# A new order of work for a cross-attention and mixture-of-experts attention kernel on one core

## What is computed

```
x = x + cross_attention(layernorm(x), ctx, lens)      # 77 context keys, 16 heads of 32, masked by length
x = x + expert_attention(layernorm(x))                # 512 keys, 16 heads of 32
```

## Time and profile before

| | |
|---|---|
| time, median of 3 runs | 1420.75 us (1419.51 to 1426.21) |
| profiled execution, span | 1426.7 us |
| PE busy | 1391.0 us, 97% of the span, 5704 matmuls |
| PE weight loads busy | 702.4 us, 49% |
| DVE, ACT, POOL busy | 67%, 60%, 48% |
| PE's granted clock, in tenths over 40 slices | 9 or more in all but two, which have 8 |

### The profile page before, as it was taken

The page is one execution under the profiler, slowest core; times in us unless marked ns, Lnnn a source line. Parts: engine busy times, 40 slices in busy tenths (PEclk is TensorE's granted clock), DMA queues, the critical chain, the costliest instruction groups (busy, mean ns, idle before and its releaser), DMA issues.

```text
span 1426.7 us, 17122 instructions
## 1 busy us (share of the span) xinstructions
PE 1391.0 (97%) x5704; PEld 702.4 (49%) x5704; DVE 951.9 (67%) x1687; ACT 861.3 (60%) x1499; POOL 679.8 (48%) x411
## 2 busy tenths in 40 slices
...
GB/s 252 143 53 133 46 68 96 153 76 46 98 110 108 75 54 125 137 61 76 68 111 123 75 59 135 110 85 67 58 104 152 76 46 97 64 101 79 81 39 30
DMA packets 78767, 130.81 MB, mean 92 GB/s; under 512 B 26374, under 2 KB 32134, under 8 KB 75607
## 3 DMA queue, kind: packets, MB, share of 16 engines
...
...
## 4 chain that ended last, share of the span: by engine, by line
PE 85%; ACT 7%; issue 2%; DMA 2%; POOL 2%; DVE 1%; ACTq 0%; SPq 0%; POOLq 0%
PE pj L1217 43%; PE scT L1302 9%; PE sc L1274 8%; PE acc L1331 7%; PE sc L1263 4%; PE pj L1247 2%; PE pj L1311 2%; PE scT L1295 2%; PE pj L1319 2%; PE pj L1340 2%; DMA qs<-shift 2%; PE pj L1190 1%; ACT xhat L810 1%; PE pj L1202 1%; PE pj L1211 1%
## 5 line engine op out<-in xcount | busy, mean ns | idle before, releaser
L925 ACT ACTIVATE probs<-scT 128x512 f32<-128x512 f32 x512 | 288.9, 594 | 303.9 <-PE scT L1302 300.8
L1048 DVE TENSOR_REDUCE negmax<-sc 128x1 f32<-128x512 f32 x512 | 338.0, 684 | 140.7 <-PE sc L1274 139.7
L784 POOL TENSOR_TENSOR probs_sum<-probs_sum,probs 128x1024 f32<-128x1024 f32 x128 | 300.2, 2365 | 57.4 <-ACT probs L925 57.3
L1075 DVE RECIPROCAL inv_sum<-pj 128x128 f32<-128x128 f32 x256 | 225.0, 921 | 59.9 <-PE pj L1340 39.2
L1274 PE MATMUL sc<-ks,qs 96*128 96x512 f32 x512 | 260.1, 541 | 2.4 <-DVE negmax L1048 1.6
L1217 PE MATMUL pj<-XT,Wqk 128*128 128x512 f32 x512 | 257.3, 598 | 0.6 <-DVE Wqk L1140 0.6
L1302 PE MATMUL scT<-qs,ks 99*128 99x512 f32 x512 | 250.9, 517 | 6.2 <-DMA qs<-shift 3.2
L780 POOL TENSOR_TENSOR probs_sum<-probs 128x1024 f32<-128x1024 f32 x64 | 151.4, 2372 | 173.8 <-ACT probs L925 173.8
L790 POOL TENSOR_TENSOR uv_stack<-UVS_sb,uv_stack 96x1024 fp32r<-96x1024 f32 x32 | 75.7, 2367 | 178.1 <-ACT UVS_sb L832 178.1
L1302 PEld LDWEIGHTS scT<-qs,ks 99*128 99x128 f32 x512 | 94.7, 191 | 124.5 <-ACT probs L925 60.4
L754 POOL TENSOR_TENSOR xhat<-xhat,inv_sum 128x128 f32<-128x128 f32 (+1 forms) x56 | 45.1, 806 | 207.7 <-DVE inv_sum L1075 207.7
...
## 6 DMA issues: line engine op xcount, KB each, us to landing
Wqk<-in_WmT SPq DMA_DIRECT2D x16, 1024.0 KB, 6.1
Wvo<-in_WmT SPq DMA_DIRECT2D x16, 1024.0 KB, 6.5
...
qs<-stage_lo SPq DMA_DIRECT2D x136, 64.0 KB, 2.2
qs<-qs SPq DMA_DIRECT2D x34, 256.0 KB, 3.0
X<-in_x SPq DMA_DIRECT2D x8, 1024.0 KB, 6.0
ks<-stage_lo SPq DMA_DIRECT2D x128, 64.0 KB, 2.0
ks<-ks SPq DMA_DIRECT2D x32, 256.0 KB, 3.0
```

The costliest lines, as they stand in the source:

```text
L784: nc.gpsimd.tensor_tensor(probs_sum[:, pair], probs_sum[:, pair], probs[:, kt % 2, pair], ALU.add)\
L925: nc.scalar.activation(probs[:, kt % 2, jj, :], scT[:, ST[step], :], ACT.Exp, scale=SCALE)\
L1048: nc.vector.tensor_reduce(negmax[:, 0, n:n + 1], sc[:, SC[step], :], AX.X, ALU.max, negate=True)\
L1075: nc.vector.reciprocal(inv_sum[:, INV[use], at], pj[:, PJ[left_in(full)], at])\
```

## The change

All numbers of `CALENDAR` and `OWN` are replaced. Everything below them is as it was: the same 3917 steps with the same instructions, the same `PERIOD`, buffers and rules for waits; since waits' values and banks are derived from the order, they follow it. Many of the new places come in pairs or fours a tenth apart, so that like steps stand next to each other. In the list of PE, a `sc` step followed by another `sc` was found 107 times and is now 222 times, `sT` by `sT` 95 and now 224 times, `sc` by `sT` or `sT` by `sc` 316 and now 159 times.

The core of the diff, with the kinds of step that are spoken of below:

```diff
 CALENDAR = {
...
-    "xpose": (-1734, -1732, -1712, -1710, 141, 141, 163, 163),
...
-    "uv_load": (346, 397, 524, 2882),
...
-    "cacc": (-1106, -626, -363, -44),
...
-    "wm_load": (235, 409, 224, 3285),
...
-    "qk_rows": (919, 773, 1317, 1353, 1778, 1739, 2284, 2360),
-    "qk_stack": (1003, 896, 1345, 1373, 1880, 1780, 2418, 2420),
...
-    "shift": (1339, 1901, 2375, 2899),
-    "shift_move": (1367, 1967, 2390, 2987),
...
-    "accout": (2115, 2487, 3005, 3448),
-    "den": (1871, 2376, 2959, 3434),
...
+    "xpose": (-1747.9, -1747.7, -1736.2, -1736.1, 146.2, 146.4, 166.3, 166.4),
...
+    "uv_load": (270.7, 270.8, 426.9, 2579.7),
...
+    "cacc": (-1191.3, -612.8, -383.2, -7.3),
...
+    "wm_load": (170.8, 286.2, 737.4, 3063.8),
...
+    "qk_rows": (866, 751.1, 1362.8, 1386.1, 2035.8, 1786.4, 2294.6, 2348.2),
+    "qk_stack": (866.1, 751.3, 1363, 1386.2, 2035.9, 1786.5, 2294.8, 2376.8),
...
+    "shift": (1437.1, 1944.7, 2368.7, 2831.7),
+    "shift_move": (1437.2, 1944.8, 2368.8, 2831.8),
...
+    "accout": (2117.8, 2526.2, 2900.9, 3459),
+    "den": (1870, 2418.2, 2902.8, 3505.2),
...
 OWN = {
...
-    "gate_hidden": {(0,): 247, (7,): 14443},
-    "gate_top": {(0,): 271, (7,): 14468},
...
-    "warm": {(0, 2): -989, (1, 3): -909, (2, 1): -663, (3, 4): -423, (4, 5): 71, (5, 2): 170, (6, 3): 244,
-        (7, 3): 323, (8, 2): 334, (9, 3): 555, (10, 4): 768},
...
-    "shift": {(7, 0): 15606, (7, 1): 18277, (7, 2): 19738, (7, 3): 20530},
...
-    "den": {(7, 0): 18507, (7, 1): 19738, (7, 2): 20740, (7, 3): 21892},
...
-    "divide": {(7, 0, 0): 18986, (7, 1, 0): 20855, (7, 2, 0): 21354, (7, 3, 0): 22067, (7, 3, 1): 22391,
-        (7, 3, 2): 23543, (7, 3, 3): 24079},
...
+    "warm": {(0, 2): -566.3, (1, 3): -542, (2, 1): -431.4, (3, 4): -374.9, (4, 5): 201.2, (5, 2): 218.8,
+        (6, 3): 181.5, (7, 3): 223.4, (8, 2): 176.1, (9, 3): 749, (10, 4): 684.5},
...
+    "shift": {(7, 0): 15653.5, (7, 1): 18511.1, (7, 2): 19859.8, (7, 3): 20758.4},
...
+    "den": {(7, 0): 18597.2, (7, 1): 20054.2, (7, 2): 21211.5, (7, 3): 22403.8},
...
+    "divide": {(7, 0, 0): 18970.9, (7, 1, 0): 21145, (7, 2, 0): 21799.1, (7, 3, 0): 22404, (7, 3, 1): 22977.8,
+        (7, 3, 2): 23089.1, (7, 3, 3): 23624.1},
+    "gate_hidden": {(0,): 212.4, (7,): 14459.7},
+    "gate_top": {(0,): 239.1, (7,): 14513.3},
```

More of the change, by code:

```diff
@@ L65 @@
-    "cinv": (-946, -942, -933, -931, -536, -530, -527, -519, -427, -408, -392, -304, -29, -17, -9, 19),
-    "wm_load": (235, 409, 224, 3285),
[L67 to L75, removed]
@@ L101 @@
-    "divide": (2251, 2923, 3435, 3454, 3559, 3656, 3896),
-    "out2": (3491, 3507, 3522, 3540, 3721, 3723, 3740, 3766, 3789, 3804, 3826, 3889, 3930, 3941, 3958, 3988),
-    "residual2": (3579, 3916, 3925, 4017),
+    "context": (-2133.4,),
+    "context_v": (-2041.2,),
+    "load": (-1944.5,),
+    "stats": (-1944.4, -1944.3, -1944.2, -1944.1),
+    "deviation": (-1887.7, 74.1),
+    "normalize": (-1786.8, 146.1),
+    "xpose": (-1747.9, -1747.7, -1736.2, -1736.1, 146.2, 146.4, 166.3, 166.4),
@@ new lines @@
+    "q1": (-1642.4, -1642.3, -1642.2, -1642.1, -1639.7, -1639.6, -1621.3, -1557.1, -924, -923.9, -923.8, -923.7,
+        -851.2, -699.1, -649, -648.9),
+    "q1_split": (-1642, -1511.7, -923.6, -648.8),
+    "q1_rows": (-1622.9, -1255.7, -909.5, -434.6),
+    "q1_stack": (-1619.8, -1213.6, -909.4, -319.9),
+    "pick": (270.6,),
+    "uv_load": (270.7, 270.8, 426.9, 2579.7),
+    "csc": (-1483.4, -1446, -1436.3, -1436.2, -1108.2, -1108.1, -1097, -1096.9, -629.1, -620, -589.3, -589.2,
+        -319.8, -319.7, -297.8, -297.7),
@@ new lines @@
+    "cross_shift": (-1387.9, -1037.1, -584.7, -269.6),
+    "cross_shift_move": (-1387.8, -1037, -584.6, -269.5),
+    "csT": (-1262.1, -1262, -1255.9, -1255.8, -933.5, -933.3, -909.7, -909.6, -527, -490.4, -490.3, -434.7, -125.9,
+        -125.8, -99.6, -99.5),
+    "cpv": (-1191.4, -612.9, -383.3, -7.4),
+    "cacc": (-1191.3, -612.8, -383.2, -7.3),
+    "cden": (-933.7, -566.9, -400, 12.1),
+    "cinv": (-933.6, -933.4, -933.2, -933.1, -468.4, -468.3, -468.2, -468.1, -399.9, -399.8, -399.7, -379.2, 54.6,
+        54.7, 55, 55.3),
@@ new lines @@
+    "wm_load": (170.8, 286.2, 737.4, 3063.8),
+    "cdivide": (-484.8, -468, -187.2, 54.8, 54.9, 55.2, 55.6),
+    "out1": (-9.8, -9.7, -9.6, 55.1, 36.1, 36.2, 36.3, 55.5, 62.5, 62.6, 62.7, 62.8, 73.6, 73.7, 73.8, 73.9),
+    "residual1": (55.4, 55.7, 62.9, 74),
+    "residual_bias": (1505.8,),
+    "token_sums": (146.5, 146.6, 166.5, 166.6),
+    "gate_hidden": (234.4,),
+    "gate_top": (270.5,),
+    "gate_scale": (295.8,),
+    "uv_hi": (356.2, 545.5, 607.9, 3138),
+    "uv_lo": (356.3, 545.6, 608, 3138.1),
@@ new lines @@
+    "weff": (461.9, 462, 485.8, 508.4, 595.7, 595.8, 607.7, 607.8, 737.5, 737.6, 737.7, 758.7, 3361.2, 3409.5,
+        3409.6, 3424.2),
+    "qk": (525.2, 536.6, 536.7, 536.8, 617.7, 617.8, 648.2, 677.7, 992.3, 1039.6, 1149.8, 1165.2, 1261.1, 1261.2,
+        1289.7, 1306.6, 1446.6, 1446.7, 1451.2, 1451.3, 1535.9, 1545.5, 1553.3, 1656.1, 2137, 2143.7, 2143.8,
+        2204.6, 2299.1, 2311.9, 2312.1, 2320),
+    "qk_split": (581.6, 677.8, 1292.9, 1306.7, 1451.4, 1701.6, 2204.7, 2328.1),
+    "qk_rows": (866, 751.1, 1362.8, 1386.1, 2035.8, 1786.4, 2294.6, 2348.2),
@@ new lines @@
+    "accout": (2117.8, 2526.2, 2900.9, 3459),
+    "den": (1870, 2418.2, 2902.8, 3505.2),
+    "inv": (1870.1, 1949.1, 1949.2, 1949.3, 2418.3, 2418.4, 2418.5, 2418.6, 2902.9, 2903, 2903.1, 2947.4, 3505.3,
+        3505.5, 3505.6, 3505.8),
+    "divide": (2218.1, 2526.3, 2947.5, 3505.4, 3505.7, 3505.9, 3506),
+    "out2": (3521.5, 3521.6, 3521.7, 3536.4, 3700.5, 3700.6, 3741.1, 3784.3, 3782, 3834.7, 3834.8, 3834.9, 3963.7,
+        3985.4, 3985.5, 3985.6),
+    "residual2": (3536.5, 3784.4, 3835, 3985.7),
@@ L104 @@
 }
 OWN = {
[L110 to L117, removed]
@@ L136 @@
-    "normalize": {(0, 0): -8677, (0, 1): 99, (7, 1): 14377},
-    "xpose": {(0, 0, 0): -8403, (0, 0, 1): -8371, (0, 0, 2): -8329, (0, 0, 3): -8320, (0, 1, 0): 148, (0, 1, 1): 149,
[10 rows of a table removed]
-    "csc": {(0, 0, 0): -1181, (0, 0, 1): -1167, (0, 0, 2): -1109, (0, 0, 3): -1098, (0, 1, 0): -1020,
[4 rows of a table removed]
-    "cross_shift": {(0, 0): -1074, (0, 1): -912, (0, 2): -677, (0, 3): -440, (7, 1): 13230, (7, 2): 13618,
-        (7, 3): 13991},
-    "cross_shift_move": {(0, 0): -1033, (0, 1): -911, (0, 2): -542, (0, 3): -418, (7, 1): 13249, (7, 2): 13640,
-        (7, 3): 14084},
@@ L157 @@
-    "csT": {(0, 0, 0): -1015, (0, 0, 1): -1013, (0, 0, 2): -947, (0, 0, 3): -946, (0, 1, 0): -789, (0, 1, 1): -704,
[4 rows of a table removed]
-    "cpv": {(0, 0): -794, (0, 1): -555, (0, 2): -215, (0, 3): -57, (7, 0): 13094, (7, 1): 13578, (7, 2): 13804,
-        (7, 3): 14182},
-    "cacc": {(0, 0): -574, (0, 1): -494, (0, 2): -172, (0, 3): -44, (7, 0): 13158, (7, 1): 13583, (7, 2): 13832,
-        (7, 3): 14203},
-    "cden": {(0, 0): -909, (0, 1): -557, (0, 2): -206, (0, 3): -39, (7, 0): 13277, (7, 1): 13679, (7, 2): 13796,
-        (7, 3): 14194},
@@ L205 @@
-    "qk_stack": {(7, 0, 0): 15094, (7, 0, 1): 15158, (7, 1, 0): 16330, (7, 1, 1): 16454, (7, 2, 0): 18220,
[4 rows of a table removed]
-    "v_bias": {(7, 0): 15130, (7, 1): 15159, (7, 2): 15316, (7, 3): 15444},
[12 rows of a table removed]
-    "shift": {(7, 0): 15606, (7, 1): 18277, (7, 2): 19738, (7, 3): 20530},
-    "shift_move": {(7, 0): 15635, (7, 1): 18303, (7, 2): 19756, (7, 3): 20542},
[16 rows of a table removed]
-    "psum": {(7, 0, 1, 0): 16914, (7, 0, 1, 1): 17517, (7, 0, 2, 0): 17555, (7, 0, 2, 1): 17811, (7, 0, 3, 0): 18332,
[4 rows of a table removed]
-    "accout": {(7, 0): 18747, (7, 1): 19953, (7, 2): 20646, (7, 3): 21990},
@@ new lines @@
+    "context": {(0,): -7316.4, (1,): -155.1},
+    "context_v": {(0,): -2800.6, (1,): -100.9, (7,): 12439},
+    "load": {(0,): -11654},
+    "stats": {(0, 0): -11653.9, (1, 0): 145.5, (0, 1): -11653.8, (1, 1): 145.6, (0, 2): -11112, (1, 2): 145.7,
+        (0, 3): -10877.6, (1, 3): 145.8},
+    "deviation": {(0, 0): -9832.6, (1, 0): 157.5, (0, 1): 145.4, (7, 1): 14303.8},
+    "normalize": {(0, 0): -9473.7, (0, 1): 157.3, (7, 1): 14372.4},
+    "xpose": {(0, 0, 0): -7759.7, (1, 0, 0): 247.3, (0, 0, 1): -7759.6, (1, 0, 1): 247.4, (0, 0, 2): -7759.5,
[11 rows of a table added]
@@ new lines @@
+    "pick": {(0,): 239.2, (7,): 14513.4},
+    "uv_load": {(0, 0): 239.3, (7, 0): 14513.5, (0, 1): 239.4, (7, 1): 14684.4, (0, 2): 555.5, (7, 2): 14684.5,
+        (6, 3): 14769.3, (7, 3): 14871.3},
+    "csc": {(0, 0, 0): -1904.7, (0, 0, 1): -1775.7, (0, 0, 2): -1730.9, (0, 0, 3): -1730.8, (0, 1, 0): -1125,
[5 rows of a table added]
+    "cross_shift": {(0, 0): -1422.2, (0, 1): -555.9, (7, 1): 13214.9, (0, 2): -478.6, (7, 2): 13653.1,
+        (0, 3): -387.8, (7, 3): 13962.1},
+    "cross_shift_move": {(0, 0): -1422.1, (0, 1): -555.7, (7, 1): 13215, (0, 2): -478.3, (7, 2): 13653.2,
+        (0, 3): -387.7, (7, 3): 13962.2},
@@ new lines @@
```

(22 more changed lines are left out.)

73 lines of the change are left out of this document (24 added, 49 removed), and 212 rows, old and new, of tables (CALENDAR, OWN).

## The result

The changed kernel takes 1469.34 us (median of 4 runs, 1466.97 to 1471.38); the kernel before, measured beside it, 1423.48. The ratio is 1.0322, 95% interval 1.0288 to 1.0355: slower by 46 us, and outside the predicted range, which ended at 1431. The profiled execution has a span of 1468.2 us, 41.5 more than that of before; the two profiles are compared by their spans. In the new file the lines lie 33 further down: L1250 is the product, L1307 `sc`, L1335 `sT`, L1313 `shift`, L1328 `csT`, L1373 `den`, L1382 and L1389 the gate; L737 is the load of 1 MB of weights (`wm_load`), L718 and L721 the DMAs of a key stack, L751 `uv_load`, L933 the shift rows.

A forecast was written before the change was run, and what follows sets the result against it. The prediction took the kernel as PE-bound, with no wait worth a per cent. Body +2, head -4 and tail -3.5 summed to -5.5 us, 1415 on the scale of the measured times (0.4% gain), range 1401 to 1431.

The forecast's parts named there:

- (e): Body, sc(b,3,0): key stack now queues behind uv_load and the 1 MB load; +0.4 us a sequence, between 0 and +1.0.
- (k): Tail: shift(7,2) gets its sT later, its wait for row maxima shortens; shift(6,2) loses 0.9 of cover; together -0.5 us.
- Rival 1: Shift round trip decides: (b), (c), (e) near upper ends, a sequence loses 2.6 us; 1428 to 1434 us; chance 0.2.
- (b): Body, shift(b,0) to sT(b,0,0,0): cover falls from 8.5 to 4.5 us against a 4.4 round trip; +0.3 a sequence.
- (c): Body, shift(b,2) to sT(b,2,0,0): cover falls from 5.4 to 4.4 us; taken as 0, between -0.3 and +1.3.
- (a): Body, xpose(b+1,0,2): PE's 0.66 us wait for the bank copied to XT falls to 0.3; -0.4 a sequence.
- (f): Head, gate of sequence 0: junk warm matmuls ahead of the gate steps remove waits of 1.05, 0.82 and 0.66; -2.5 us.
- (g): Head, weff(0,1) and weff(0,2): more cover for the 1.9 us uv_stack waits; -1.5 us, or nothing if uv_stack comes later.
- (i): Head, csc(0,3,0): cover falls from 10.7 to 6.6 us where 9.5 are needed; +2 us, between 0 and +3.
- (j): Tail, last job's row sums: first sum starts some 1.7 us earlier, divide(7,2) leaves the chain; up to -3.0 us.
- Rival 3: The clock: half-clock stretch at 58.4 to 82.2 us, worth some 11 us, goes if PE stays fed; 1404 us; chance 0.13.
- Rival 4: Matmul rows hide waits between unlike score steps; the pairs bring back 16 us, 1405 or less; chance 0.09.

The follow-up runs named there:

- The quarter load: The changed kernel, same order, with wm_load(b,1) cut to a quarter (256 KB instead of 1 MB) for all sequences but the first: 1418.80 us, ratio 0.9941.
- the reversed experiment: The kernel before with only wm_load(b,1) moved ahead of the key stack qk_stack(b-1,3,1), for all sequences: 1450.97 us, ratio 1.0173.

## Why the prediction was wrong

The step that failed is (e): "0 if the stack lands before, +1.0 if it queues behind the load. I take +0.4." It had the change (wm_load now ahead of the key stack), the row (1 MB, 6.1 us to land) and the place. What it measured is 5.9 us a sequence in waits alone, 35 in six; its own sign, that `sc` waits for a stack's DMA, came. The error was to add the load as one more landing to a chain, with 11.6 us of cover beside it. What stands in front of the stack is bytes on engines that are busy already: at 217 GB/s the 14 us of the window are 3.0 MB, the load, the factors, the stack and the rest. A DMA of 256 KB behind them lands in 6.3 to 8.9 us and not in 3.0, and the load in 9.3 to 11.3 and not in the 6.1 of the row. (e) also had one thing wrong in the old order: of its two `uv_load` one stood ahead of the stack there too, at 420.19 in the timeline of before; the other one and the load changed places with it. The quarter load shows the size of it, the reversed experiment shows that one move of the load does this to the old order too, and the load behind the stack takes 53 us off the changed kernel. By that the range of (e) should have gone up to the load's whole landing, 6 us a sequence.

Its second half is in (k): "shift(6,2) loses a cover of 0.9", with the rest for -0.5. There the load stood ahead of the shift rows of sequence 6, and their wait is 10.0 us instead of 1.1. The wait for row maxima at shift(7,2), which (k) had shorter, is 2.1 instead of 1.9.

Rival 1, the slower side, named (e) as a third of its mechanism and stopped at 0.7 for it. The shift rows of (b) and (c), its other two thirds, did next to nothing: (c) waits at most 0.5 in sequences 0 to 5, 1.2 in all where it was 2.1 (0 was taken), and (b) 1.0 in one sequence of six (0.3 a sequence was taken). (d) waits 0.6 once, at `sT(6,3)`. (a) is right, and more: 4.0 of waits for XT became 0.5.

In the head (f) is right. The gate of sequence 0 after the change, the waits of the earlier trace rows gone:

```profile
113.26 2.40 PE L1215 MATMUL acc<-Wq_sb,ident_sb 128*128 128x128 f32 x20
115.57 1.02 PE L1382 MATMUL pj<-pooled,gw1T_sb 128*128 128x1 f32 x8
116.45 1.36 PE L1215 MATMUL acc<-Wq_sb,ident_sb 128*128 128x128 f32 x10
117.65 0.29 PE L1389 MATMUL pj<-gw2T_sb,hiddenB 128*128 128x8 f32 x2
117.80 2.04 PE L1244 MATMUL pj<-ident_sb,xhat 128*128 128x128 f32 x12
```

(g) is right in size: 0.4 is left of 1.9. (i) was wrong in its place: `csc(0,3,0)` does not wait, but `csT(0,0,0)` does, 2.5 us, for its shift rows, once more behind a load of 1 MB, that I had not looked for there. (h) was not read by itself.

In the tail (j) is right: the first of the six sums starts 4.6 us after `sT(7,3,0,0)` instead of 5.6, the sums run on without the divide, and `den` waits no more than 0.1:

```profile
1439.11 4.70 POOL L813 TENSOR_TENSOR probs_sum<-probs 128x1024 f32<-128x1024 f32 x2 [0.57 <-PE pj L1373]
...
1443.77 9.30 POOL L817 TENSOR_TENSOR probs_sum<-probs_sum,probs 128x1024 f32<-128x1024 f32 x4
...
1453.22 1.06 PE L1373 MATMUL pj<-probs_sum,ones 128*32 128x512 f32 x8
```

From `sT(7,3,0,0)` to the end of the last product it is 30.4 us instead of 33.3. The stretch before it, from `sc(7,2,0)`, is 4 us longer (43.4 against 39.5), so the tail gains nothing in sum; what is at fault there was not tried.

Rival 2 fell with the result. Rival 3 asked whether the order sets the half clock at 58 to 82 us: see below. Rival 4 does not show: with the load behind the stack a sequence is 0.4 to 1.5 us shorter than before, 1.0 on the mean, of which the waits for XT are some 0.66; the 16 us of this rival would be 2 for each of the eight.

What stays open: whether the DMA engines themselves or the memory behind them set the 217 GB/s, and whether the load issued from ScalarE's queue would let SyncE's small ones pass. That was not tried; that ScalarE's shift rows were as late behind SyncE's load as SyncE's stack speaks against it. The Trainium skill says so too, in "DMA: Bandwidth & Descriptors", section "Issuing engines are not separate DMA queues": all of them end up on the same 16 engines. The trace agrees, with the 10.0 us of ScalarE's shift rows at `sT(6,2)`.
